# Dealing the slots of projections, output tiles and norms anew in a Mamba-2 scan kernel

## The reference

```python
zxbcdt = u @ in_proj_w.T                       # z 1024, x 1024, B 128, C 128, dt 64
xBC = silu(causal_conv(xBC, 4 taps) + conv_b)
dt = softplus(dt_raw + dt_bias); dA = dt * -exp(A_log)
# in chunks of 64 tokens, 64 heads of 16 columns:
Y_diag = (C B^T * L) (x dt)                    # L = exp of differences of the running sums of dA
states = B^T (decay * x dt)
prev   = prev * chunk_decay + states           # a chain over the chunks
Y_off  = C prev * exp(dA_cum)
y  = (Y_diag + Y_off + x * D) * silu(z)
yn = y * rsqrt(mean(y*y) + eps) * norm_weight
x1 = layernorm(u + yn @ out_proj_w.T)
out = layernorm(x1 + rmsnorm(down(silu(gate(x1)) * up(x1))))     # fp4 weights
```

## Time and profile before

| | |
|---|---|
| Time, median of 3 runs | 1935.93 us (1935.18 to 1938.17) |
| The profiled execution's own time | 1932.81 us |
| Its span, first to last instruction | 1931.0 us |
| Mean granted TensorE clock | 0.926 of full |
| Busy: PE, DVE, ACT, POOL | 1701.7, 1373.8, 937.8, 1007.3 us |
| Chain that ended last | PE 57%, DVE 23%, issue 10%, SPq 3%, ACT 3%, DMA 2% |
| Batch 3's body, from 597.6 to 761.0 us | 163.40 us: PE busy 144.20, DVE 113.84, ACT 68.96, POOL 76.59, clock 0.89 |
| Batch 2's body, from 437.4 to 597.6 us | 160.20 us: PE busy 140.40, DVE 114.41, clock 0.91 |
| Last body without the next projection, from 1245.58 to o3 at 1354.06 us | 108.48 us |

### The profile page before, as it was taken

The page is one execution under the profiler, slowest core; times in us unless marked ns, Lnnn a source line. Parts: engine busy times, 40 slices in busy tenths (PEclk is TensorE's granted clock), DMA queues, the critical chain, the costliest instruction groups (busy, mean ns, idle before and its releaser), DMA issues.

```text
span 1931.0 us, 37015 instructions
## 1 busy us (share of the span) xinstructions
PE 1701.7 (88%) x11168; PEld 878.3 (45%) x11168; DVE 1373.8 (71%) x2200; ACT 937.8 (49%) x1647; POOL 1007.3 (52%) x1031
## 2 busy tenths in 40 slices
PE   2687989898888888988888888978899999999998
PEld 1244545444444454554454455455344444444443
DVE  6858657858766875785776687596677777777775
ACT  3463263435335325343533533532676666666662
POOL 0045435526544552562654365286577776767774
PEclk9898898889899879889989987987999999999999
DMA  6111140123014113112301411362011111111111
GB/s 210 48 48 26 36 98 21 40 53 86 25 42 107 28 35 75 46 38 52 88 25 42 101 30 39 86 179 46 33 39 50 34 55 51 33 49 55 33 34 55
DMA packets 214679, 109.66 MB, mean 57 GB/s; under 512 B 133796, under 2 KB 185696, under 8 KB 214496
## 3 DMA queue, kind: packets, MB, share of 16 engines
q1 hardware_dynamic: 214496, 107.37, 21.2%
HBM read 80.57 MB, written 26.76 MB: 56 GB/s over the span
## 4 chain that ended last, share of the span: by engine, by line
PE 57%; DVE 23%; issue 10%; SPq 3%; ACT 3%; DMA 2%; DVEq 1%; POOL 0%; ACTq 0%; POOLq 0%
PE ps_in L794 13%; PE ps_in L772 8%; PE ps_in L926 7%; PE ps_yo L941 6%; PE ps_yd L941 6%; PE ps_yo L852 5%; DVE pre L1271 5%; PE ps_s L926 4%; PE ps_t L926 4%; DVE mix L1358 3%; DVE state L1373 2%; PE ps_t L819 1%; PE ps_d L830 1%; DVE res L1426 1%; DMA lhs_d<-ld_dram 1%
## 5 line engine op out<-in xcount | busy, mean ns | idle before, releaser
L1077 ACT ACTIVATE decay<-ps_d 128x512 f32<-128x512 f32 x256 | 151.7, 593 | 320.3 <-PE ps_d L830 258.7
L772 PE MATMUL ps_in<-u_hi,w_hi 128*128 128x512 f16 (+1 forms) x608 | 235.4, 387 | 58.2 <-DVE u_lo L1258 36.3
L1358 DVE TENSOR_TENSOR mix<-decay,gb 128x512 f32<-128x512 f32 x256 | 226.9, 892 | 51.3 <-PE ps_yd L842 17.7
L1659 POOL TENSOR_TENSOR xend<-xpad,decay 128x256 f32<-128x256 f32 x256 | 185.0, 742 | 145.4 <-PE ps_yo L865 116.8
L794 PE MATMUL ps_in<-w_out,zg 128*128 128x512 f32 x512 | 254.3, 654 | 6.1 <-DVE pre L1271 6.1
L772 PE MATMUL ps_in<-u_hi,w_lo 128*128 128x512 f16 (+1 forms) x608 | 235.4, 387 | 0.0
L772 PE MATMUL ps_in<-u_lo,w_hi 128*128 128x512 f16 (+1 forms) x608 | 235.3, 387 | 0.0
L1751 POOL TENSOR_TENSOR gate_sum<-gate_sum,gate_part 128x512 f32<-128x512 f32 x88 | 142.3, 1617 | 101.7 <-DVE gate_part L1580 101.3
L1271 DVE SCALAR_TENSOR_TENSOR pre<-ps_in,cws,pre 128x511 f32<-128x511 f32 (+2 forms) x240 | 178.9, 746 | 8.6 <-ACT pre L1016 2.8
L794 PEld LDWEIGHTS ps_in<-w_out,zg 128*128 128x128 f32 x512 | 108.3, 218 | 133.8 <-issue 125.0
L852 PE MATMUL ps_yo<-bc,state 128*128 128x64 f32 x896 | 152.2, 341 | 18.0 <-DVE state L1373 17.9
(11 more groups left out here) (181 smaller groups left out, 3775.7 us busy)
## 6 DMA issues: line engine op xcount, KB each, us to landing
ebc<-e_dram SPq DMA_DIRECT2D x256, 64.0 KB, 2.7
u<-u_t SPq DMA_DIRECT2D x9, 1024.0 KB, 5.3
res<-u_tok SPq DMA_DIRECT2D x32, 256.0 KB, 2.7
x_dram<-res SPq DMA_DIRECT2D x32, 256.0 KB, 2.0
xa<-x_dram SPq DMA_DIRECT2D x8, 1024.0 KB, 5.7
xr<-x_dram SPq DMA_DIRECT2D x32, 256.0 KB, 2.6
out<-xr SPq DMA_DIRECT2D x32, 256.0 KB, 2.0
fw_words<-gu_words SPq DMA_DIRECT2D x32, 176.0 KB, 3.6
```

What stands on the lines that cost most here:

```text
L772: last = mm(ps_in[bk][0:m, :], w[:, k, col:col + m], u[:, k, :], start=(k == 0 and j == 0), stop=(k == KT - 1 and j == 2))
L1077: ac(decay[:, n % NG, :, :].rearrange("p a b -> p (a b)"), ps_d[n % 2][:, :], ACT.Exp).then_inc(e_done, 1)
L1358: v.tensor_tensor(mix[:, n % NG, :, :], decay[:, n % NG, :, :], gb[:, c % 2, 0:CH].unsqueeze(1).broadcast_to([P, CT, CH]), ALU.mult).then_ ...
L1659: g_.tensor_tensor(xend[:, pairs, :], xpad[:, c % 2, pairs, :], decay[:, g, :, CH - 1:CH].broadcast_to([P, CT, 2 * HD]), ALU.mult).then_in ...
```

## The change

The slots are dealt anew. The output tiles o0, o1, o2 go from slots 14, 22, 30 to 12, 20, 28, the first of chunks 3, 5 and 7, and their q's from 12, 20, 28 to 13, 21, 29, behind the tile. Chunks 3, 5 and 7 hold no projection. dt, B and C go to slots 4, 5 and 7 (chunk 1), x0 and x1 to 9 and 11, x2 and x3 stay at 17 and 19, x4 and x5 are at 25 and 27, x6 goes to the tail in front of x7. norm_tile of o0 to o2 stands three slots behind the tile (NORM_AT), norm_tile_end five (NORM_END); that of o2 falls behind x6's and x7's taps in the tail. The splits of u take slots 1 and 2 instead of 1 to 4. dt's parts, exp_dt, exp_cs and ln_dt move with dt. decode of units 0 and 1 goes from slots 21 to 29 to slots 29 and 30. In SP's program store_parts goes from slot 25 to 26, load_head from 30 to 29, store_x1 and load_res of a tile to slot 18 and 26. In the last body, which has no projection, output tiles, q's and norms move in the same way.

```diff
-DT_SLOT = {9: 0, 11: 1, 13: 2, 17: 3, 19: 4}
-SPLIT_SLOT = {k + 1: (k,) for k in range(KT)}
+DT_SLOT = {7: 0, 9: 1, 13: 2, 17: 3, 21: 4}
+SPLIT_SLOT = {1: (0, 1), 2: (2, 3)}
+NORM_AT, NORM_END = 3, 5
...
-TAIL = {"pro": ["x7", "z0"] + HEAD, "body": ["x7", "z0", "o3", "q3"] + HEAD, "last": ["o3", "q3"]}
+TAIL = {"pro": ["x7", "z0"] + HEAD, "body": ["x6", "x7", "z0", "o3", "q3"] + HEAD, "last": ["o3", "q3"]}
...
-BODY_USES = [(5, "dt"), (7, "B"), (9, "C"), (11, "x0"), (12, "q0"), (14, "o0"), (15, "x1"), (17, "x2"),
-             (19, "x3"), (20, "q1"), (22, "o1"), (23, "x4"), (25, "x5"), (27, "x6"), (28, "q2"), (30, "o2")]
-LAST_USES = [(12, "q0"), (14, "o0"), (20, "q1"), (22, "o1"), (28, "q2"), (30, "o2")]
+BODY_USES = [(4, "dt"), (5, "B"), (7, "C"), (9, "x0"), (11, "x1"), (12, "o0"), (13, "q0"), (17, "x2"), (19, "x3"),
+             (20, "o1"), (21, "q1"), (25, "x4"), (27, "x5"), (28, "o2"), (29, "q2")]
+LAST_USES = [(12, "o0"), (13, "q0"), (20, "o1"), (21, "q1"), (28, "o2"), (29, "q2")]
...
-        DECODE_AT = {"body": {21: [(0, 0), (0, 1)], 25: [(0, 2), (0, 3)], 27: [(1, 0), (1, 1)], 29: [(1, 2), (1, 3)]},
+        DECODE_AT = {"body": {29: [(0, part) for part in range(4)], 30: [(1, part) for part in range(4)]},
...
-                    if n == 25 and st.proj is not None:
+                    if n == 26 and st.proj is not None:
                         store_parts(b + 1)
-                    if n == 30 and st.proj is not None:
+                    if n == 29 and st.proj is not None:
                         load_head(b + 1)
...
-                        if f"o{tt}" in st.at(n):
+                        if f"o{tt}" in st.at(n - NORM_END - 1):
                             store_x1(b, tt)
                             load_res(b, tt + 2)
-                    if "o2" in st.at(n):
-                        store_x1(b, 2)
+                store_x1(b, 2)
                 store_x1(b, 3)
...
-                    if st.proj is not None and n == 7:
+                    if st.proj is not None and n == 6:
                         exp_dt(st.proj)
-                    if st.proj is not None and n == 20:
+                    if st.proj is not None and n == 23:
                         exp_cs(st.proj)
                         ln_dt(st.proj)
...
-                    for tt in range(TT - 2):
-                        if f"o{tt}" in st.at(n - 2):
+                    for tt in range(TT - 1):
+                        if f"o{tt}" in st.at(n - NORM_AT):
+                            norm_tile(st, tt)
+                        if f"o{tt}" in st.at(n - NORM_END):
                             norm_tile_end(st, tt)
                     if st.proj is not None:
-                        if n == 6:
+                        if n == 5:
                             dt_first(st)
                         if n in DT_SLOT:
                             dt_second(st.proj, DT_SLOT[n])
-                        if n == 23:
+                        if n == 25:
                             dt_third(st.proj)
...
-                norm_tile_end(st, TT - 2)
...
-                use_in(st, SLOTS)
+                use_in(st, SLOTS, "x")
+                norm_tile_end(st, TT - 2)
+                use_in(st, SLOTS, "o")
...
-                        if n > 0 and f"o{tt}" in st.at(n - 1):
+                        if f"o{tt}" in st.at(n - NORM_AT - 1):
                             ln_root(b, tt)
                 gate(st, NC - 1)
+                ln_root(b, TT - 2)
```

More of the change, by code:

```diff
@@ L1118, in tail @@
                         take_conv(st, name)
+                    if name == CONV_TILES[-1]:
                         if st.kind == "body":
@@ L1427, in norm_tile_end, with use_in @@
                                 ALU.subtract, ALU.mult).then_inc(x1_done, 1)
-            def use_in(st, slot):
+            def use_in(st, slot, only=""):
                 for name in st.at(slot):
+                    if only and name[0] != only:
+                        continue
                     if name in CONV_TILES:
@@ L1437, in use_in @@
                             mean_square(st, TT - 1)
-                        norm_tile(st, int(name[1]))
+                            norm_tile(st, TT - 1)
             def turn(f, par, tiles):
```

## The result

The changed kernel takes 1890.53 us (median of 4 runs, 1888.63 to 1896.46), the kernel before on the same chip 1935.56 us: ratio 0.9771, with a 95% interval of 0.9756 to 0.9787. It is 45 us faster; I had forecast 103. The profiled execution of after is the longest of its four, 1896.46 us with a span of 1894.7, against 1931.0 before.

A forecast was written before the change was run, and what follows sets the result against it. No engine is full; TensorE and VectorE wait for each other in turns. Seven bodies at -14.3 us (steps -11.6, tail -2.7) and -3 for the last, -103 from 1932.8, gave 1833 us by the median; 8-in-10 range 1787 to 1885.

The forecast's parts named there:

- Step 3-4: Batch 3, from the start of chunk 3's yoff multiplication to chunk 4's; 21.35 us before, forecast 13.9.
- signs that I had named: Tile within 4 us of yoff, VectorE's tile wait under 2, steps 14-17 and 12-15, clock above 0.85, bodies 15 us shorter.
- tile steps: Steps 2-3, 4-5 and 6-7, yoff to yoff: set by TensorE at 14.7, 14.7 and 13.9 us, 46.3 with clock loss.
- plain steps: Steps without an output tile, 3-4 and 5-6: 13.9 and 13.3 us, together 27.2, bounds 26.1 and 31.1.
- sign of being wrong: Long within or from_before waits, clock near 0.7 with a tile, steps without one over 18 us, or ps_t holding TensorE at slot 25.
- low end: Steps 2-3, 4-5 and 6-7 with no price for the clock: 43.3 us for the three.
- upper end: Steps 3-4 and 5-6 with one more long mix and ScalarE's block holding TensorE: 31.1 us together.
- Tail: End of a body, from the last yoff to tile o3: 12.5 us instead of 15.22, saving 2.7.
- Head: Start of a body, dt in slot 4 and earlier splits: change of 0, between -2 and +2 us.
- The last body: Body without projections: five steps and the stretch to o3 take 79 us against 80.5, put at -3.
- SP's queue: store_parts ahead of store_x1(1) and load_res(3): the next body's rows come no later, load_res(3) still has time.
- third case: Clock swing stays, 52.3 us with tiles, and 31.1 without: about 1900 us; one alone 1870 to 1885; chance 0.17.

The follow-up runs named there:

- second experiment: The kernel after with norm_tile_end of o0 and o1 four slots later (21 and 29 instead of 17 and 25) and the stores of x1 behind it: 1892.54 us.
- first experiment: The kernel after with exp_cs and ln_dt back in ScalarE's slot 20 and dt's part 4 back in VectorE's slot 19: 1894.31 us.
- first combination: The kernel after with dt's part 3 in slot 13, decodes and dt_third in 29, exp_cs and ln_dt in 28, store_parts in 30, load_head in 31: 1822.59 us.

## Why the prediction was right and wrong

**Bound and mechanism: right.** Both engines did wait for each other in turns, and evening out the steps is what gained. Step 3-4 went from 21.35 to 15.40 us and 5-6 from 21.99 to 15.30. The kernel with the tiles alone has 33 of the 45 us. VectorE no longer stands for a tile in front of norm_tile (4.36 and 6.64 us in before, 0.49 and 0.44 in after, and those for GpSimd's root). While a tile runs it stands 1.3 us at most in 2-3 and 4-5; in 6-7 it is 4.35 us for the product behind the tile, over the 2 us that I had named. Of the signs that I had named, tile steps of 14 to 17 us came (15.1 to 16.3); plain steps of 12 to 15 didn't, by 0.3 to 0.4 us, nor a clock above 0.85 in each step (0.79 and 0.78 in 4-5 and 5-6), nor 15 us less a body. One sign of being wrong appeared: ps_t holds TensorE at slot 25, for 3.75 us, though that did not set the step.

**Tile steps: right, 1.1 us too low.** 47.4 against 46.3 us. The value near the low end was fair: the two tiles with a half-clock start paid 1.7 and 2.0 us, from_before nothing, where I had allowed 1.0 a step for both. Step 6-7 paid nothing to the clock and was still 1.2 us over its own sum of 13.9: o2 starts 5.33 us after yoff (684.89 - 679.56), behind TensorE's own projection, and not 3.69. The rule of the Trainium skill that I had set against the rows (TensorE: Matmul & The Clock Gate, "A second HAM failure mode: psum-queue depth-cycling") would have made them 52.3: this trace agrees that small gaps between groups bring half clock, since it did so in two tiles of three, but the three steps are 4.1 us over the sum without it and not 9.0.

**Plain steps: the term that failed most, 27.2 forecast, 30.7 measured.** The step of the prediction is "21.35 less 4.36 and 0.90 of idle, less one set of taps", and the same for 5-6. It took VectorE's operations at the durations that they had in before. In 3-4 the 13.8 were 12.4 us of work (14.70 less 2.3) and 1.4 of small waits; measured are 14.24 of work and 1.2 of waits. The waits were right, the work was not: with the taps gone, the same operations took longer (and q0's mean square, 0.15, came in). In 3-4 the four mix took 0.74 us more in all, norm_tile_end 0.44 (2.23 against 1.78) and dt's part 3 0.52; in 5-6 mix 0.99, norm_tile_end 0.42 and dt_third 1.14. That is 4.2 us in the two steps. GpSimd is busy 12.54 of the 15.40 us, and the one of them that was tested, norm_tile_end, loses by standing beside it (second experiment); for mix and dt's pieces this is argued from that. I had named the upper end for it, 31.1, "one such mix more" and ScalarE's block. The size of that end was right, one reason for it was wrong: the block didn't set step 5-6 (first experiment). Nor did I ask which of VectorE's pieces could leave a step that it sets: 3.2 us of dt in 3-4 and 3.1 us of dt_third in 5-6 could.

**Tail: the other term that failed, 12.5 forecast, 14.96 measured.** The sum put "x6 and x7 2.6 each" at full clock. x6 took 5.28 us until ScalarE had it, behind a wait that my own sum contained (4.1 us from yoff; measured 3.89). With the clock held up the tail is 12.52: the other terms were right in sum. In the tile steps I had put a price on the clock after a wait, in the tail I forgot it.

**Head: "both about cancel", 0.7 too low.** Before the first yoff it got 0.19 us shorter (19.53 to 19.34), well inside the bound of -2. The early splits earn no more than that by themselves, but dt's earlier slot needs them: without them the stretch is 23.26. Step 1-2 got 0.86 longer. The prediction charged it with "dt part 0 into slot 7"; part 0 stood in this step before too, in slot 9. What came in is part 1, which the prediction had taken out of step 2-3 and never added here, and a second set of taps. With part 1 out again the step is 14.99.

**The last body** gained 1.9 us and not 3. The stretch that was forecast, from chunk 2's yoff to o3, did gain 3.2 (80.50 to 77.26); its head, which had no term, lost 1.3 (27.98 to 29.32). **SP's queue:** none of the waits in these steps was ended by a late store or load, as argued.

**Sum.** Of the 8.1 us a body that are missing in batch 3, plain steps are 3.5, the tail 2.5, tile steps 1.1, the head 0.7, the stretch from o3 0.4. About one more comes from taking batch 3 as the measure: it was 163.4 us before, the mean of batches 1 to 6 162.1, and after 157.2 and 157.0. The result lies in the forecast's third case, between its 1885 for one mechanism and its 1900 for both; that case's first mechanism, tile steps at 52.3, isn't what happened, its second, plain steps at their upper end, is.

## What to carry to other kernels

Before forecasting a reordered schedule, sum each engine's work for each new step with the small pieces in it, and ask which of those can move into a step where that engine waits; here one such move of 3.2 us gave 38 us, and the first combination, with two of them and the decodes, is 68 us faster than after, where the whole change gave 45. Take an operation's duration from the place where it will stand, and not from where it stood. Taking a wait away shortens its step only if that wait sets the step: with the longest one (3.75 us) removed step 5-6 stayed, and a wait came up in the next step. Price the clock behind every wait that a new order leaves in front of a long group of matmuls.

## What the runs showed of the hardware

- **VectorE loses time beside GpSimd by place.** In after norm_tile_end runs 32 times. The fifteen beside GpSimd's state_d take 2.22 or 2.23 us, the fifteen with no operation of GpSimd beside them 0.54 or 0.55, the other two, beside others, 0.68 and 0.85. The one at 641.60 began 0.51 us after state_d and ended 0.29 us behind it (643.83 against 643.54), and the other fourteen ended likewise 0.3 us behind. Put another operation there and it takes 2.23 us as well. The Trainium skill, SBUF — State Buffer, section "Who interferes with whom", says that VectorE's operations with two inputs in SBUF contend with a GpSimd instruction that reads SBUF, and that in a 2-port mode, which an operation like this TENSOR_SCALAR can enter under conditions, whoever issues first gets the shared pair of ports for the whole instruction and the other fully blocks. These rows agree with the order: GpSimd's began first, and VectorE's ended behind it. They don't show a full block, since what is left behind state_d, 0.29 us, is less than the 0.54 that the operation takes alone.
- **The same wait does not always lower the clock.** In after, a wait of 1.92 us in front of o0 of batch 3 is followed by a tile of 8.80 us. In the first experiment, whose first edit lies seven slots behind o0, the same wait is followed by a tile of 7.11 us. TensorE's timeline of that kernel:

```profile
625.32 7.11 PE L794 MATMUL ps_in<-w_out,zg 128*128 128x512 f32 x16 [1.92 <-DVE pre L1272]
```

  So a tile step has two lengths, 15.96 and 14.26 us, behind the same wait in the same order of work. In the first experiment both occur in one execution: batch 1's step 2-3 is 15.96 us, those of batches 2 to 6 are 14.26 or 14.27. With the wait filled by 8 unread matmuls steps 2-3 and 4-5 of batches 1 to 6 are all 14.26 or 14.27. What decides where the wait isn't filled no run here separates.
- **16 unread matmuls of 3.63 us together kept the clock up through a wait** and made a kernel with more work 19 us faster.
